# Mean-embedding projection: where block 5 is loaded, how many weight blocks load before the hold, and which engine empties the banks until tile 2 joins

## The chip, the cores and the metric

The kernel runs on one core of a Trainium2 chip. The metric is the device time of one execution in microseconds (us). It works with five engines: TensorE (PE, with PEld for its weight loads), VectorE (DVE), ScalarE (ACT), GpSimd (POOL) and SyncE (SP), which here only issues DMAs.

## The reference

```python
valid = sequence_ids < emb_table.shape[0]          # 1024 x 200 ids, 12500 items
safe_ids = jnp.where(valid, sequence_ids, 0)
seq_emb = emb_table[safe_ids] * valid[..., None]   # rows of 512 floats
denom = jnp.maximum(valid.sum(axis=1, keepdims=True), 1.0)
user_repr = seq_emb.sum(axis=1) / denom            # 1024 x 512
logits = user_repr @ proj_w + proj_b               # 512 x 12500, bias of 12500
```

The ids are drawn between 35 and 109962, so that only about 23 of a user's 200 ids are valid. The result is 1024 x 12500 floats.

## The kernel before

**Tiles and units.** The 1024 users are 8 tiles of 128. The weights are cut into 25 blocks of 500 columns (1000 KB each). The product of one block and one tile is a *unit*: 12 matmuls of 128x500 (high half of the mean by high half of the weights, high by low, low by high, four parts of 128 rows each) into one of six PSUM banks. There are 200 units, and TensorE runs them in the order of the list `units`, counted by `r`. Units are done as tiles become ready: tile 0 alone for r = 0 to 9, tile 1 *joins* at r = 10, tile 2 at 22, tile 3 at 35, tile 4 at 51 (`joined`). Blocks are counted by `q` from 0 to 46, because a tile that joins late needs the first blocks again.

**Means.** For each tile GpSimd gathers 26 *columns* (row c of each of 128 users, `gather`, L353) and one more for the rest into a ring of 12 buffers `rows`. Columns are summed by VectorE (`add_column`, L561), and for the first three tiles also by TensorE (`sum_column`, L791): all 26 of tile 0, columns 18 to 25 of tile 1 (numbers 44 to 51), 24 and 25 of tile 2 (76 and 77). TensorE's columns of tile t come at r = joined[t] - 2; then ScalarE scales the part from PSUM (`rest_share`, L449), VectorE finishes the mean (`mean_of`, L607), and TensorE turns it (`turn`, L763) at r = joined[t] - 1, between two units.

**Weights.** SyncE loads a raw block q into a slot (`load_w`, L289), ScalarE makes its high half (`w_high`, L422), VectorE the low half (`w_low`, L625, two instructions, after which the raw slot is free). Block 0 to 4 are prepared ahead; block q >= 5 at the step `split_due[q]`: blocks 5 to 10 at r = 1 to 6, 11 to 14 at r = 11 to 14, 15, 16, 17 at r = 23, 24, 25, 18 at 36. Slots: two in `w_raw` (slots 0, 1), two in the area of the means (`raw_at_hi`, `raw_at_lo`, slots 2, 3), and one in `stage`, used once (slot 4, block 4). From block 16 (`MORE_LOADS`) only slots 0 and 1 are used. A load waits (`raw_last`) for the low half of the block that had its slot before. The loads of `first_loads` (q = 0 to 8) are issued ahead of the unit loop; from q = `LATE_LOAD` = 7 on they are held until the last column of tile 0 has landed. Later loads are issued at the step where the block before in their slot is split.

**Leaving the banks.** A finished unit is copied to `stage` and stored. It leaves by ScalarE if `by_act[r]` (L413, and then TensorE adds the bias with a thirteenth matmul, L847, from `bias_parts`), else by VectorE (L640, which adds `bias_sb`, a ring of four bias blocks that SyncE loads from step `BIAS_DUE` = 3). `by_act` holds for all r below joined[ACT_TILES] = 10 and for the even r below 65. Unit r waits until unit r - 6 has left its bank.

Each engine does its instructions in the order written. In VectorE's loop at step r: `move_out(r)` if it is its unit, `fill_slots` at a join (it waits for TensorE's `list_rest`, L775 to L777, behind that unit), `w_low`, `mean_of`, and the columns due at r. In ScalarE's loop `w_high` comes ahead of `move_out(r)`. In SyncE's loop at step r: bias loads at `BIAS_DUE`, store(r), weight loads, bias loads of a slot that comes free.

Of the kernel before, what the change touches and what calls it, by code (L numbers as in the profile page):

```python
# [5 lines left out]
def mean_embedding_projection(nc, ids, table, proj, bias, out, FAST=26,  # L6
# [9 lines left out]
    K = HID // P  # L16
# [10 lines left out]
    RAW, SPLIT, BIAS, ROWS, PLACED, BANKS = 2, 5, 4, 12, 2, 6  # L27
# [1 line left out]

    ON_PE, DIAGS = ((0, FAST), (18, FAST), (24, FAST)), 4  # L30
    RAW_MORE, MORE_LOADS = 2, 16
    FURTHER_BEHIND, LIST_FIRST_AT, BIAS_DUE = 20, 21, 3
    ACT_TILES, BOTH_TILES = 1, 5
    PART_AT = (0, 32, 64)
    BIAS_ROWS = PART_AT[-1] + NB
    COLS = FAST * TILES
# [15 lines left out]
    LOADS = start[-1] + NB  # L52
# [8 lines left out]
    UNITS = len(units)  # L61
    assert UNITS == TILES * NB
    first_unit = [min(r for r, (x, _) in enumerate(units) if x == q) for q in range(LOADS)]
    last_unit = [max(r for r, (x, _) in enumerate(units) if x == q) for q in range(LOADS)]
    joined = [min(r for r, (_, x) in enumerate(units) if x == t) for t in range(TILES)]
    stores, at = [], 0
    for q, first, n in steps:
# [19 lines left out]
                      for t in range(TILES)]  # L87
    assert all(by_pe[FAST * t + j] is False and j >= FAST - ROWS for t, j in enumerate(further_behind) if t)
    GATHER_LEAD = 5
    LATE_LOAD, REST_FIRST_AT, OPENED = 7, 18, SPLIT - 1  # L90

    def column_due(c):

# [5 lines left out]


    ONCE = RAW + RAW_MORE
    raw_slot = [q if q <= ONCE else (q - 1) % ONCE if q < MORE_LOADS else q % RAW for q in range(LOADS)]
    raw_turn = [sum(raw_slot[x] == raw_slot[q] for x in range(q + 1)) for q in range(LOADS)]
    raw_last = [max((x for x in range(q) if raw_slot[x] == raw_slot[q]), default=None) for q in range(LOADS)]
    assert MORE_LOADS < JOIN[TILES // 2] and RAW_AT + BW <= (STAGE - K) * BW

    split_due = [None] * SPLIT + [min(last_unit[q - SPLIT] + 1, first_unit[q] - 1) for q in range(SPLIT, LOADS)]

    w_view = proj.rearrange("(k p) n -> p k n", p=P)
# [5 lines left out]
    with ctx:  # L115
        def sb(name, shape, dt):
            return ctx.enter_context(nc.sbuf_tensor(name, shape, dt))

        def sem(name):
            return ctx.enter_context(nc.semaphore(name))  # L120
# [63 lines left out]
        bias_sb = sb("bias_sb", [P, BIAS, BW], F32)  # L184
# [49 lines left out]
        s_fb_rows = sem("branch_rows_gathered")  # L234
        s_pool_passed = sem("pool_passed")
        s_dve_passed = sem("dve_passed")
        s_raw = [sem(f"w_loaded{i}") for i in range(RAW + RAW_MORE + 1)]
        s_bias = [sem(f"bias_loaded{i}") for i in range(BIAS)]
        s_w_hi = sem("w_hi_ready")
        s_w_lo = sem("w_lo_ready")  # L240
# [24 lines left out]
        def wait_moved(engine, r):  # L265

            engine.wait_ge(s_moved_by_act if by_act[r] else s_moved_by_dve, nth_moved[r] + 1)
# [5 lines left out]
        def raw(q):  # L273
            if raw_slot[q] == ONCE:
                return raw_once
            return w_raw[:, raw_slot[q]] if raw_slot[q] < RAW else raw_more[raw_slot[q] - RAW][:]

        def diagonal_of(c):
# [5 lines left out]
        @block.sync  # L284
        def _(sp):
            def load_w(q):
                if raw_last[q] is not None:
                    sp.wait_ge(s_w_lo, raw_last[q] + 1)
                sp.dma_start(raw(q), w_view[:, :, bass.ts(q % NB, BW)]).then_inc(s_raw[raw_slot[q]], 16)  # L289

            def load_bias(i):

                if i >= BIAS:
                    wait_moved(sp, late_last[i - BIAS])
                sp.dma_start(bias_sb[:, i % BIAS], bias_view[late[i] % NB:late[i] % NB + 1].to_broadcast([P, BW])).then_inc(
                    s_bias[i % BIAS], 16)

            def store(g):
                r, q, first, n = stores[g]
                wait_moved(sp, r + n - 1)  # L300
                sp.dma_start(out_view[:, first:first + n, bass.ts(q % NB, BW)],
                             stage[:, g % STAGE, 0:n]).then_inc(s_stored[g % STAGE], 16)

            sp.dma_start(ids_sb[:, 0], ids_view[:, 0]).then_inc(s_ids0, 16)
            sp.dma_start(ids_sb[:, 1:], ids_view[:, 1:]).then_inc(s_ids, 16)
            for q in range(RAW):
                load_w(q)
            sp.wait_ge(s_bias_zero, 1)
            for at in PART_AT:
                sp.dma_start(bias_raw[at:at + NB], bias_view).then_inc(s_bias_raw, 16)  # L310
            first_loads = [q for q in range(LOADS) if raw_last[q] is None or raw_last[q] < SPLIT]
            for q in first_loads[RAW:]:
                if q == LATE_LOAD:
                    sp.wait_ge(s_rows[(FAST - 1) % ROWS], 16 * ((FAST - 1) // ROWS + 1))
                load_w(q)
            sp.wait_ge(s_bias_parts, 3)
            for r in range(UNITS):
                if r == BIAS_DUE:
                    for i in range(BIAS):
                        load_bias(i)  # L320
                for g in range(len(stores)):
                    if stores[g][0] + stores[g][3] - 1 == r:
                        store(g)
                for q in range(len(first_loads), LOADS):
                    if split_due[raw_last[q]] == r:
                        load_w(q)
                for i in range(BIAS, len(late)):
                    if r == late_last[i - BIAS]:
                        load_bias(i)
            for i in range(STAGE):  # L330
                sp.wait_ge(s_stored[i], 16 * len(range(i, len(stores), STAGE)))
# [63 lines left out]
        def _(act):  # L395
# [20 lines left out]
            def w_high(q):  # L416
                if q >= SPLIT:
                    act.wait_ge(s_product, last_unit[q - SPLIT] + 1)
                if q == SPLIT - 1:
                    act.wait_ge(s_added, len(pe_columns[0]))  # L420
                act.wait_ge(s_raw[raw_slot[q]], 16 * raw_turn[q])
                nc.scalar.activation(w_hi[:, q % SPLIT], raw(q), ACT.Copy).then_inc(s_w_hi, 1)  # L422
# [71 lines left out]
        def _(dve):  # L494
# [120 lines left out]
            def w_low(q):  # L615
                dve.wait_ge(s_w_hi, q + 1)
                half = K // 2
                for h in range(2):
                    at = h * half
                    if q < OPENED:  # L620
                        dve.wait_ge(s_opened, 2 * q + h + 1)
                        high = acc[:, at:at + half, 0:BW]
                    else:
                        high = w_hi[:, q % SPLIT, at:at + half].bitcast(F32)
                    low = dve.tensor_tensor(w_lo[:, q % SPLIT, at:at + half], raw(q)[:, at:at + half], high, ALU.subtract)  # L625
                    if h:
                        low.then_inc(s_w_lo, 1)
                    elif q < OPENED:
                        low.then_inc(s_half_low, 1)
# [242 lines left out]
```

## Time and profile before

| what | value |
|---|---|
| median of 3 runs | 638.0 us (637.69 to 638.16) |
| the profiled execution, its own time | 639.96 us |
| its span, first to last instruction | 638.1 us |
| PE busy | 609.2 us (95%) |
| DVE busy | 407.6 us (64%) |
| ACT busy | 145.6 us (23%) |
| POOL busy | 231.1 us (36%) |
| mean granted TensorE clock | 0.997 of full speed |

The busy time of an engine is read over the span. The matmuls are pipelined and their ends are modelled, so that a busy TensorE may still have small gaps. Times within the profile count from the first instruction. The profiled execution took 1.96 us longer than the median of the runs.

### The profile page before, as it was taken

What the parts mean: (1) busy time and instruction counts of PE and PEld (TensorE: products, weight loads), DVE (VectorE), ACT (ScalarE), POOL (GpSimd) and SP (SyncE); (2) the same over time, 40 slices, a digit from 0 to 9 for tenths busy, and PEclk for the clock granted to TensorE, in tenths of its full rate; (3) what the DMA queues carried; (4) which work ended last, traced back from release to release, by engine and by line L of the source; (5) the groups of instructions that cost most, each with busy time, mean ns of one, the idle gap of its engine ahead of it and who ended that gap; (6) DMA issues with size and microseconds to landing.
All of it is one profiled execution on the core that took longest, in us unless ns stands there. A gap on an engine that the chain in (4) does not pass through costs nothing.

```text
span 638.1 us, 7597 instructions
## 1 busy us (share of the span) xinstructions
PE 609.2 (95%) x2602; PEld 477.3 (75%) x2602; DVE 407.6 (64%) x723; ACT 145.6 (23%) x161; POOL 231.1 (36%) x227
## 2 busy tenths in 40 slices
PE   1989889989999999999999999999999999999997
PEld 0337558768788787788888888888888888888886
DVE  7988949899878898697885554332333333344442
ACT  8917425132122131300200221111011111211210
POOL 5777877777763767566550000000000000000000
PEclk9998999999999999999999999999999999999999
DMA  9979999999997999798893398454555555566632
GB/s 310 387 257 342 385 394 344 358 303 324 315 302 267 311 302 315 238 325 248 253 339 114 99 293 283 123 168 163 173 167 174 177 178 177 175 191 202 218 127 103
DMA packets 77704, 158.31 MB, mean 248 GB/s; under 512 B 9288, under 2 KB 65043, under 8 KB 77659
## 3 DMA queue, kind: packets, MB, share of 16 engines
q1 hardware_dynamic: 60378, 110.30, 51.1%
q0 software_dynamic: 17280, 47.47, 22.9%
q8 instruction: 21, 0.34, 0.2%
q14 instruction: 25, 0.20, 0.1%
HBM read 115.70 MB, written 51.20 MB: 262 GB/s over the span
## 4 chain that ended last, share of the span: by engine, by line
PE 72%; DVE 19%; issue 5%; DMA 2%; DVEq 1%; ACT 0%; POOL 0%; POOLq 0%
PE acc L842 70%; DVE sums L561 7%; DVE w_lo L625 5%; DMA rows<-in_L_rec_emb_table_dram,index 2%; DVE key L518 1%; DVE top L514 1%; DVE stage L640 1%; PE acc L847 1%; DVEq L259 1%; DVE index L516 0%; PE turned L763 0%; PE turned L783 0%; DVE mean L607 0%; DMA ids_sb<-in_r_sequence_ids_dram 0%; DVE key L502 0%
## 5 line engine op out<-in xcount | busy, mean ns | idle before, releaser
L353 POOL DMA_INDIRECT rows<-in_L_rec_emb_table_dram,index x208 | 221.6, 1066 | 96.3 <-issue 55.8
L842 PE MATMUL acc<-w_hi,mean_hi 128*128 128x500 f32 x800 | 225.3, 403 | 0.8 <-ACT mean_hi L438 0.8
L640 DVE TENSOR_TENSOR stage<-acc,bias_sb 128x500 f32<-128x500 f32 x162 | 109.3, 676 | 179.2 <-PE acc L842 179.1
L842 PE MATMUL acc<-w_lo,mean_hi 128*128 128x500 f32 x800 | 214.6, 390 | 0.0
L842 PE MATMUL acc<-w_hi,mean_lo 128*128 128x500 f32 x800 | 213.7, 389 | 0.4 <-DVE mean_lo L612 0.3
L842 PEld LDWEIGHTS acc<-w_hi,mean_hi 128*128 128x128 f32 x800 | 150.7, 190 | 32.0 <-issue 4.3
L842 PEld LDWEIGHTS acc<-w_lo,mean_hi 128*128 128x128 f32 x800 | 150.8, 189 | 31.5
L842 PEld LDWEIGHTS acc<-w_hi,mean_lo 128*128 128x128 f32 x800 | 150.3, 188 | 32.1 <-DVE mean_lo L612 1.2
L561 DVE SCALAR_TENSOR_TENSOR sums<-rows,mask,sums 128x512 f32<-128x512 f32 x165 | 124.0, 752 | 16.2 <-issue 8.2
L422 ACT ACTIVATE w_hi<-w_raw 128x2000 fp32r<-128x2000 f32 x39 | 72.9, 1875 | 235.3 <-PE acc L842 215.8
L625 DVE TENSOR_TENSOR w_lo<-w_raw,w_hi 128x1000 fp32r<-128x1000 f32 x74 | 85.3, 1194 | 13.6 <-ACT w_hi L422 13.6
L413 ACT ACTIVATE stage<-acc 128x500 f32<-128x500 f32 x38 | 22.2, 587 | 79.9 <-PE acc L847 79.8
L449 ACT ACTIVATE rest_mean<-turned,inv_count 128x512 f32<-128x512 f32 x7 | 4.8, 690 | 78.3 <-PE turned L783 68.9
L791 PE MATMUL turned<-rows,diags_at_hi 128*128 128x512 f32 x30 | 15.9, 688 | 1.4 <-DMA rows<-in_L_rec_emb_table_dram,index 1.4
L514 DVE MAX8 top<-key 128x8 f32<-128x200 f32 x40 | 14.6, 366 | 0.7
L791 PE MATMUL turned<-rows,diag 128*128 128x512 f32 x20 | 10.8, 638 | 4.3 <-DMA rows<-in_L_rec_emb_table_dram,index 2.4
L847 PE MATMUL acc<-bias_parts,pick 89*128 89x500 bf16 x38 | 14.6, 385 | 0.0
L518 DVE MATCH_REPLACE8 key<-top,key 128x200 f32<-128x200 f32 x40 | 14.1, 353 | 0.0
L791 PEld LDWEIGHTS turned<-rows,diags_at_hi 128*128 128x128 f32 x30 | 6.5, 224 | 10.0 <-issue 7.3
L438 ACT ACTIVATE mean_hi<-turned 128x512 fp32r<-128x512 f32 x8 | 4.8, 598 | 32.4 <-PE turned L763 32.4
L797 PE MATMUL acc<-many,ones_b 128*128 128x16 bf16 x1 | 0.2, 194 | 12.4 <-DVE stage L659 12.4
L791 PEld LDWEIGHTS turned<-rows,diag 128*128 128x128 f32 x20 | 3.1, 188 | 11.9 <-DMA rows<-in_L_rec_emb_table_dram,index 11.8
(106 smaller groups left out, 193.1 us busy)
## 6 DMA issues: line engine op xcount, KB each, us to landing
out_dram<-stage SPq DMA_DIRECT2D x200, 250.0 KB, 3.9
w_raw<-in_L_rec_proj_w_dram SPq DMA_DIRECT2D x39, 1000.0 KB, 6.6
bias_sb<-in_L_rec_proj_b_dram SPq DMA_DIRECT2D x39, 250.0 KB, 4.9
raw_at_hi<-in_L_rec_proj_w_dram SPq DMA_DIRECT2D x4, 1000.0 KB, 11.6
rows<-in_L_rec_emb_table_dram,index POOLq DMA_INDIRECT x208, 6.0
raw_at_lo<-in_L_rec_proj_w_dram SPq DMA_DIRECT2D x3, 1000.0 KB, 15.2
stage<-in_L_rec_proj_w_dram SPq DMA_DIRECT2D x1, 1000.0 KB, 26.1
ids_sb<-in_r_sequence_ids_dram SPq DMA_DIRECT2D x1, 700.0 KB, 4.4
```

The source lines that it names most:

```text
L259: return engine.value_load(need[0:1, t + TILES:t + TILES + 1], min_val=0, max_val=MORE)
L353: return pool.indirect_dma_start(out=dst, out_offset=None, in_=table, in_offset=bass.IndirectOffsetOnAxis(ap=column, axis=0), bounds_check ...
L413: nc.scalar.activation(stage[:, g % STAGE, r - stores[g][0]], acc[:, r % BANKS, 0:BW], ACT.Copy).then_inc(s_moved_by_act, 1)
L422: nc.scalar.activation(w_hi[:, q % SPLIT], raw(q), ACT.Copy).then_inc(s_w_hi, 1)
L514: dve.max(eight, key[:]).then_inc(s_sort, 1)
L518: dve.match_replace(key[:], eight, key[:], -1.0).then_inc(s_sort, 1)
L561: dve.scalar_tensor_tensor(sums[:], rows[:, c % ROWS], mask[:, t, j:j + 1], sums[:], ALU.mult, ALU.add).then_inc(s_summed, 1)
L625: low = dve.tensor_tensor(w_lo[:, q % SPLIT, at:at + half], raw(q)[:, at:at + half], high, ALU.subtract)
L640: dve.tensor_tensor(stage[:, g % STAGE, r - stores[g][0]], acc[:, r % BANKS, 0:BW], bias_sb[:, i % BIAS], ALU.add).then_inc(s_moved_by_dve, 1)
L791: nc.tensor.matmul(turned[:], diagonal_of(c), rows[:, c % ROWS], start=j == 0, stop=j == FAST - 1).then_inc(s_added, 1)
L842: last = nc.tensor.matmul(bank, first, second, start=part + k == 0, stop=part == 2 and k == K - 1 and not by_act[r])
L847: last = nc.tensor.matmul(bank, pick[:, q % NB:q % NB + 1].to_broadcast([BIAS_ROWS, P]), bias_parts[:], start=False, stop=True)
```

## The change

The four bias buffers `bias_sb` (128 x 4 x 500 floats, as large as a raw block) become a sixth raw slot (`IN_BIAS` = 5), used once, for block 5. Blocks 6 to 15 take slots 0 to 3 in turn from slot 0 on. In the table below are the slots before and after, and which block's low half a load waits for.

| block | 5 | 6 | 7 | 8 | 9 | 10 | 11 | 12 | 13 | 14 | 15 | 16 | 17 | 18 |
|---|---|---|---|---|---|---|---|---|---|---|---|---|---|---|
| slot before | 0 | 1 | 2 | 3 | 0 | 1 | 2 | 3 | 0 | 1 | 2 | 0 | 1 | 0 |
| waits for, before | 0 | 1 | 2 | 3 | 5 | 6 | 7 | 8 | 9 | 10 | 11 | 13 | 14 | 16 |
| slot after | 5 | 0 | 1 | 2 | 3 | 0 | 1 | 2 | 3 | 0 | 1 | 0 | 1 | 0 |
| waits for, after | none | 0 | 1 | 2 | 3 | 6 | 7 | 8 | 9 | 10 | 11 | 14 | 15 | 16 |

`LATE_LOAD` goes from 7 to 8. `ACT_TILES` goes from 1 to 2, so that ScalarE empties all banks below r = 22: the six units 11, 13, 15, 17, 19 and 21 move to it, and TensorE adds their bias. The first bias loads come at r = 16 (22 - 6) in place of r = 3, after a wait for block 5's low half. 39 bias loads become 35.

```diff
-    FURTHER_BEHIND, LIST_FIRST_AT, BIAS_DUE = 20, 21, 3
-    ACT_TILES, BOTH_TILES = 1, 5
+    FURTHER_BEHIND, LIST_FIRST_AT = 20, 21
+    ACT_TILES, BOTH_TILES = 2, 5
...
-    LATE_LOAD, REST_FIRST_AT, OPENED = 7, 18, SPLIT - 1
+    LATE_LOAD, REST_FIRST_AT, OPENED = 8, 18, SPLIT - 1
...
-    raw_slot = [q if q <= ONCE else (q - 1) % ONCE if q < MORE_LOADS else q % RAW for q in range(LOADS)]
+    IN_BIAS = ONCE + 1
+    raw_slot = [q if q <= IN_BIAS else (q - 2) % ONCE if q < MORE_LOADS else q % RAW for q in range(LOADS)]
...
+    assert BIAS == K
...
-        s_raw = [sem(f"w_loaded{i}") for i in range(RAW + RAW_MORE + 1)]
+        s_raw = [sem(f"w_loaded{i}") for i in range(IN_BIAS + 1)]
...
+            if raw_slot[q] == IN_BIAS:
+                return bias_sb[:]
...
-                if r == BIAS_DUE:
+                if r == joined[ACT_TILES] - 6:
+                    sp.wait_ge(s_w_lo, IN_BIAS + 1)
                     for i in range(BIAS):
                         load_bias(i)
```

## Rows read from the trace of the kernel before

**Rows 1.** Page, part 1: busy us (share of the span) xinstructions
```profile
PE 609.2 (95%) x2602; PEld 477.3 (75%) x2602; DVE 407.6 (64%) x723; ACT 145.6 (23%) x161; POOL 231.1 (36%) x227
```
**Rows 2.** Waits of PE over the span: us in total, times, longest
```profile
PE turned L791 <- DMA rows<-in_L_rec_emb_table_dram,index: 4.3, 7, 1.4
PE turned L763 <- DVE mean L607: 2.7, 3, 1.8
...
PE acc L842 <- DVE mean_lo L612: 0.3, 1, 0.3
```
**Rows 3.** Chain that ended last: start us, us, what
```profile
80.46 5.97 DMA rows<-in_L_rec_emb_table_dram,index
86.47 1.12 PE turned L791 x2
...
354.23 280.57 PE acc L842 x1236
```
**Rows 4.** Timeline of POOL: start us, us, engine line op [idle before]
```profile
80.46 1.00 POOL L353 DMA_INDIRECT rows<-in_L_rec_emb_table_dram,index  x1 [0.30 <-issue]
```
**Rows 5.** Timeline of PE, 47 to 88 us
```profile
47.07 0.66 PE L763 MATMUL turned<-ident,mean 128*128 128x128 f32 x4 [1.49 <-DVE mean L600]
48.50 2.00 PE L842 MATMUL acc<-w_hi,mean_hi 128*128 128x500 f32 x4 [0.78 <-ACT mean_hi L438]
...
52.83 1.26 PE L842 MATMUL acc<-w_hi,mean_hi 128*128 128x500 f32 x4
...
55.78 1.25 PE L842 MATMUL acc<-w_hi,mean_hi 128*128 128x500 f32 x4
...
76.48 2.09 PE L791 MATMUL turned<-rows,diag 128*128 128x512 f32 x4 [1.83 <-ACT diag L406]
```
**Rows 6.** Windows of PE around 49 us: us, busy, clock, DMA share, GB/s
```profile
50.00:51.00 1.00, 1.00 (x4) 0.50 1.03 391
```
**Rows 7.** Timeline of DVE
```profile
46.26 0.75 DVE L600 SCALAR_TENSOR_TENSOR mean<-turned,inv_count,rest_mean 128x512 f32<-128x512 f32 x1
...
88.46 0.75 DVE L607 SCALAR_TENSOR_TENSOR mean<-sums,inv_count,rest_mean 128x512 f32<-128x512 f32 x1 [6.47 <-ACT rest_mean L449]
...
109.01 0.67 DVE L640 TENSOR_TENSOR stage<-acc,bias_sb 128x500 f32<-128x500 f32 x1
109.60 2.30 DVE L625 TENSOR_TENSOR w_lo<-w_raw,w_hi 128x1000 fp32r<-128x1000 f32 x2
```
**Rows 8.** Timeline of DVE, 137 to 170 us
```profile
137.62 0.21 DVE L576 TENSOR_SCALAR rank<-turned,own_slot 128x1 f32<-128x1 f32 x1
...
141.26 2.30 DVE L625 TENSOR_TENSOR w_lo<-raw_at_hi,w_hi 128x1000 fp32r<-128x1000 f32 x2
...
150.07 2.30 DVE L625 TENSOR_TENSOR w_lo<-w_raw,w_hi 128x1000 fp32r<-128x1000 f32 x2
...
169.40 0.75 DVE L607 SCALAR_TENSOR_TENSOR mean<-sums,inv_count,rest_mean 128x512 f32<-128x512 f32 x1
```
**Rows 9.** Timeline of PE, 130 to 171 us
```profile
130.35 0.66 PE L763 MATMUL turned<-ident,mean 128*128 128x128 f32 x4 [1.81 <-DVE mean L607]
...
136.91 0.36 PE L777 MATMUL turned<-before,select 128*128 128x1 f32 x2
...
170.20 0.66 PE L763 MATMUL turned<-ident,mean 128*128 128x128 f32 x4 [0.73 <-DVE mean L607]
```
**Rows 10.** Timeline of ACT: high half of block 17
```profile
143.79 1.87 ACT L422 ACTIVATE w_hi<-w_raw 128x2000 fp32r<-128x2000 f32 x1
```
**Rows 11.** Landing of block 15's load, issued at 103.12 us
```profile
DMA to landing us min/median/max: 7.4/7.4/7.4
```
**Rows 12.** Landing of block 7's load, issued at 43.35 us
```profile
DMA to landing us min/median/max: 6.9/6.9/6.9
```
**Rows 13.** Landing of block 17's load, issued at 115.67 us
```profile
DMA to landing us min/median/max: 10.1/10.1/10.1
```
**Rows 14.** Landing of column 25's gather, issued at 40.30 us
```profile
DMA to landing us min/median/max: 3.0/3.0/3.0
```
**Rows 15.** Landing of all 39 loads into `w_raw`, whole span
```profile
DMA to landing us min/median/max: 5.1/6.6/18.9
```

## The prediction

> **What bounds the kernel now.** I read the page's first part, then TensorE's waits, then the chain that ended last, and then the timelines of each engine around the places that these name. TensorE is busy for 95% of the span [rows 1], and from 354 us on the chain is nothing but its unit matmuls [rows 3]: every microsecond that TensorE loses before 170 us, and does not lose already, is added to the end. TensorE's own waits after the first unit are few [rows 2]: 4.3 us for gathered rows and, at the joins, 2.7 us for the mean of VectorE, 0.3 us for a low half. So a gain can come from three places only: the stretch from 73 to 87 us, where TensorE sums columns 44 to 51 of tile 1; the 1.81 us in front of tile 2's turn at 130.35; and 0.73 us in front of tile 3's at 170.20 [rows 9]. At the first place the reader is to see that column 51 is gathered at 80.46 with GpSimd never idle but for the 0.30 us of its issue [rows 4], and that its landing 5.97 us later is what TensorE waits for [rows 3]. VectorE meanwhile idles 6.47 us ahead of tile 1's mean [rows 7]: it is not the bound there. Between 137 and 169 us VectorE has no gap except one of its own registers; it is late for tile 3, and what delays it there delays TensorE.
>
> **Part 1: block 5 in the bias buffers, eight blocks ahead of the hold.** One more megabyte stands in SyncE's queue while tile 0's last columns are gathered. Column 25, issued at 40.30, landed in 3.0 us because the queue had run empty [rows 14]; with the queue busy the nearest row is column 51's, 5.97 us [rows 3]. So column 25 lands by 46.3 in place of 43.3, TensorE ends tile 0's sum 1.1 us behind it (as it does behind column 51 [rows 3]), at 47.4, and the first mean, at 46.26 now [rows 7], starts up to 1.2 us later (0 if the queue empties in time). The held loads, at 43.35 now [rows 12], go as much later, but block 7 is no longer among them. What hides the 1.2 us: TensorE reaches column 44 with 1.83 us to wait [rows 5], and the columns behind it are bound by GpSimd's steady pace, and VectorE has its 6.47 us. I cost it at 0; without that cover it is +1.2.
>
> Blocks 6 to 9 come earlier, and the four bias loads leave the stretch from 61 to 77 us. ScalarE gets blocks 9 and 10 without waiting, so that the diagonals are not late. But the last column decides: its issue is GpSimd's pace, and its landing changes only if SyncE's queue is empty at 80 to 86 us. Blocks 10 to 14 are still issued from 61 to 78 us, each released by VectorE's split of an earlier one, and five stores between them: 6.3 MB. At half of the 391 GB/s that the DMA engines move when full [rows 6] these are 32 us, until 93; even with the light gathers of columns 46 to 51 leaving SyncE's queue two thirds, 24 us, until 85 or 86. An estimate, but the queue is busy until about when the last columns land. So I take 0, with bounds -3.0 (from the latency of column 25 [rows 14]) and 0.
>
> The Trainium skill (DMA: Bandwidth & Descriptors, Queues, rings and completion order) says that each DMA engine goes round the queues that have work, packet by packet. By that rule the depth of SyncE's queue does not matter to a gather, only whether anything is in it: the gain is 0 as long as one block is left, as in my sum; if latency went by the backlog, the two megabytes less would bring part of the 3.0 us. No row here tells the two apart.
>
> **Part 2: six units by ScalarE.** Each adds one bias matmul. An all-ScalarE unit takes 55.78 - 52.83 = 2.95 us [rows 5]; a unit without it 280.57 x 12 / 1236 = 2.72 us [rows 3]. So +0.22 us each, five of them (1.1 us) ahead of tile 2's turn, the sixth behind it. From VectorE go six moves, 0.59 us each from start to start [rows 7], five ahead of tile 2's mean: 2.95 us, of which I take back 0.35 because block 11's low half then has to wait for its high half. Tile 2's mean is ready about 2.6 us earlier and TensorE comes 1.1 us later, so its 1.81 us wait vanishes: turn at 130.35 - (1.81 - 1.1) = 129.64. The sixth bias costs 0.22 and the 0.3 us wait for the low mean [rows 2] goes: at unit 23 TensorE is 0.79 us ahead. ScalarE's six moves of about 0.6 us each fall into its idle time.
>
> **Part 3: block 17 has lost its early slot.** This is nothing that the change is named for. Before, block 17 waited for block 14's low half and was issued at 115.7 [rows 13]. Now blocks 15 and 17 share slot 1, and 17 can't be issued before VectorE has split block 15 at r = 23, two steps before 17 itself is due at r = 25. On SyncE it stands behind store 23, which is no later than that. Step by step:
> - `fill_slots` at r = 22 now starts at 137.62 without a gap [rows 8]; it waits for TensorE's list, which ended at 136.91 + 0.36 = 137.27 [rows 9] and comes 0.79 earlier. VectorE can start at 136.5: 1.1 us ahead, no more, whatever it saved before.
> - Block 15's low half ends at 141.26 + 2.30 - 1.1 = 142.5. Load 17 is issued then.
> - Its landing: block 15's load went out with the queue almost empty among heavy gathers, as this one will: 7.4 us [rows 11]. Bounds 6.9 [rows 12] and 10.1 [rows 13]. At 7.4 it lands at 149.9.
> - ScalarE's high half takes 1.87 us [rows 10]: until about 151.8. `w_low(17)` starts at 151.9 in place of 150.07 [rows 8]: +1.8, where it would have been 1.1 ahead. A stall of 2.9 us.
> - Behind it on VectorE stand the rest of tile 3's columns, then moves 27, 29, 31 and the mean at 169.40 [rows 8], with no gap to take it up. The mean is 1.8 us late, and tile 3's turn goes from 170.20 to 172.0. Behind `w_high(17)` on ScalarE stands move 26, which TensorE wants only for unit 32.
> - TensorE, 0.79 ahead, waits 0.73 + 0.79 + 1.8 = 3.3 us there.
>
> By the bounds of the landing this part ends at +1.3 or +4.5 against before; I take +1.8. It already contains all that part 2 gave.
>
> **The clock.** The first unit ran at 1.2 GHz for a while: the granted clock fell to 0.50 [rows 6] after TensorE had been idle for 1.49 and 0.78 us with 0.66 us of transposes between [rows 5]. That unit took 52.83 - 48.50 = 4.33 us in place of 2.95: 1.4 us lost. The clock stayed at 2.4 GHz after the 1.81 us gap at 130. The new gap, 3.3 us, is longer than both. Bounds 0 and +1.4; nearest row: +1.4.
>
> **The sum.** 0 + 1.8 + 1.4 = +3.2 us. In the profiled execution's own time that is 639.96 + 3.2 = 643.2; against the median of the runs, which lies 1.96 us below it, 638.0 + 3.2 = 641.2 us. Behind 172 us nothing changes: the later slots are the same, and VectorE follows TensorE's lists, so that the delay is neither grown nor given back.
>
> **The rivals.**
> - *Block 17 late, but the clock holds*: 638.0 + 1.8 = 639.8. For it: three gaps of up to 1.8 us left the clock alone.
> - *SyncE's queue runs empty before column 51's landing* (not slower): TensorE starts unit 8 up to 3.0 us earlier and everything shifts with it: 641.2 - 3.0 = 638.2, and 636.8 if the clock holds. It decides where the queue drains before 80 us. For it: two megabytes less in front of it by then; against: loads 13 and 14 go out at 74 and 78 us.
> - *Block 17 is hidden* (faster): if it landed within 7.4 - 2.9 = 4.5 us of its issue VectorE would not wait; then only part 2 is left: 0.79 + 0.73 at most, some 638.0 - 1.2 = 636.8. Against: the fastest load of a block in `w_raw` in the whole trace landed in 5.1 us [rows 15].
> - *The start passes through*: if the 1.2 us of the first mean are not covered, 641.2 + 1.2 = 642.4. Against: 1.83 us of waiting and a gather pace that does not depend on it.
>
> **How the numbers follow.** Late block with clock fall 0.41; with clock kept 0.21; queue empty 0.18 (half of it at 638.2, half at 636.8); block 17 hidden 0.08; start passes through 0.12. About 0.2% (1.3 us) is what a measurement here can tell from no change. Slower: 0.41 + 0.12 and most of 0.21, allowing for small errors of the terms (0.14): 0.67. Same: the other 0.07, 0.09 at 638.2, and part of the 636.8 cases: 0.21. Faster: 0.12. The range runs from 637.4, which takes in the queue case with the fall, to 642.6, which takes in the start and a landing of block 17 of 8.8 us; what is left out is the two cases at 636.8 and a landing of 10 us, below 0.2. The likeliest case by itself, with the clock's bounds: 639.3 to 642.6.
>
> **What would show it.** In the profile after: load 17 issued at about 142.5 and ScalarE's `w_hi` near 150 waiting for that DMA; VectorE idle some 2.9 us ahead of `w_lo` of block 17; no wait at tile 2's turn, 3.3 us at tile 3's, and a clock of 0.5 behind it; 44 bias matmuls; column 51 landing near 86.4 and unit 8 starting near 87. If unit 8 starts near 84, part 1 is wrong; if VectorE does not wait near 150, part 3 is.

## The result and the profile after

| | before | after |
|---|---|---|
| median | 638.08 us (637.69 to 638.2, 4 runs) | 643.84 us (642.85 to 644.34, 4 runs) |
| profiled execution, own time | 639.96 us | 642.85 us |
| its span | 638.1 us | 641.1 us |

The change makes the kernel slower: 1.0085 times the time before, with an interval of 1.007 to 1.01. The forecast was 641.2 us, slower. The direction is right, the time lies 1.2 us above the top of the range.

The page of after, part 1 (busy us, share of the span, instructions), beside [rows 1]:

```profile
PE 610.7 (95%) x2608; PEld 477.6 (74%) x2608; DVE 404.2 (63%) x717; ACT 148.7 (23%) x167; POOL 230.5 (36%) x227
```

Six moves went from VectorE to ScalarE, and TensorE has its six more bias matmuls. TensorE's waits in after, beside [rows 2]:

```profile
PE turned L796 <- DMA rows<-in_L_rec_emb_table_dram,index: 6.6, 9, 1.2
PE turned L768 <- DVE mean L612: 4.3, 1, 4.3
...
PE turned L768 <- DVE mean L605: 0.9, 1, 0.9
...
PE acc L847 <- DVE mean_lo L617: 0.2, 1, 0.2
```

Before, the mean at L607 was waited for three times, 2.7 us in all. After, it is waited for once, for 4.3 us: one wait that takes the place of the two at tiles 2 and 3. The timeline of TensorE in after says where, beside [rows 9] (start us, us, engine line op [idle before]):

```profile
86.25 1.46 PE L847 MATMUL acc<-w_hi,mean_hi 128*128 128x500 f32 x4
...
128.64 0.60 PE L768 MATMUL turned<-ident,mean 128*128 128x128 f32 x4
...
171.86 0.66 PE L768 MATMUL turned<-ident,mean 128*128 128x128 f32 x4 [4.34 <-DVE mean L612]
172.28 1.88 PE L847 MATMUL acc<-w_hi,mean_hi 128*128 128x500 f32 x4
173.96 1.87 PE L847 MATMUL acc<-w_lo,mean_hi 128*128 128x500 f32 x4
```

The chain that ended last leads from there back to the load of block 17 (start us, us, what):

```profile
139.03 2.31 DVE w_lo L630 x2
141.36 8.51 DMA w_raw<-in_L_rec_proj_w_dram
149.95 1.89 ACT w_hi L427
151.90 1.08 issue
152.98 1.19 DVE w_lo L630
```

It is to be read as one sentence: block 15's low half ends at 141.36, in that moment load 17 is issued, it takes 8.51 us, ScalarE makes the high half, VectorE the low half. In [rows 8] VectorE began this low half at 150.07 without having waited. In after it idled 3.95 us first (timeline of VectorE):

```profile
151.86 2.31 DVE L630 TENSOR_TENSOR w_lo<-w_raw,w_hi 128x1000 fp32r<-128x1000 f32 x2 [3.95 <-ACT w_hi L427]
```

Behind the wait TensorE's clock is down for a while. Windows of TensorE in after (stretch, us, busy, granted clock, DMA share, GB/s):

```profile
165.00:170.00 5.00, 2.52 (x12) 1.00 0.91 318
170.00:175.00 5.00, 3.14 (x11) 0.74 0.96 300
175.00:180.00 5.00, 5.00 (x24) 0.92 0.76 261
```

So far the chain is as forecast, link by link; the landing took 8.5 us where 7.4 had been taken. What does not fit is the amount: 642.85 - 639.96 = 2.9 us between the two profiled executions, but 643.84 - 638.08 = 5.8 us between the medians. The experiments had to say why, and whether block 17 is really all of it.

### The profile page after: what moved, and what is told of

Same layout as the page of the kernel before. It is cut to its first block, busy times and chain, and to the rows that moved or that the text cites. A ratio compares the mean times of both kernels' runs of the same rounds, so it can differ in the third digit from the quotient of the medians.

```text
span 641.1 us, 7605 instructions
## 1 busy us (share of the span) xinstructions
PE 610.7 (95%) x2608; PEld 477.6 (74%) x2608; DVE 404.2 (63%) x717; ACT 148.7 (23%) x167; POOL 230.5 (36%) x227
## 4 chain that ended last, share of the span: by engine, by line
PE 82%; DVE 8%; DMA 5%; issue 3%; ACT 1%; POOL 0%; DVEq 0%; POOLq 0%; ACTq 0%
PE acc L847 77%; DVE sums L566 3%; PE turned L796 3%; DMA rows<-in_L_rec_emb_table_dram,index 3%; DVE w_lo L630 2%; DMA w_raw<-in_L_rec_proj_w_dram 1%; PE acc L852 1%; PE turned L788 1%; ACT w_hi L427 1%; DVE key L523 1%; PE turned L768 1%; DVE top L519 0%; DMA ids_sb<-in_r_sequence_ids_dram 0%; DVE count L657 0%; DVE stage L645 0%
## 5 line engine op out<-in xcount | busy, mean ns | idle before, releaser
L645 DVE TENSOR_TENSOR stage<-acc,bias_sb 128x500 f32<-128x500 f32 x156 | 105.1, 675 | 183.7 <-PE acc L847 183.6
L630 DVE TENSOR_TENSOR w_lo<-w_raw,w_hi 128x1000 fp32r<-128x1000 f32 x74 | 85.2, 1193 | 14.2 <-ACT w_hi L427 14.1
L418 ACT ACTIVATE stage<-acc 128x500 f32<-128x500 f32 x44 | 25.8, 587 | 79.9 <-PE acc L852 79.9
L852 PE MATMUL acc<-bias_parts,pick 89*128 89x500 bf16 x44 | 17.0, 386 | 0.0
L852 PEld LDWEIGHTS acc<-bias_parts,pick 89*128 89x128 bf16 x44 | 4.5, 101 | 11.0 <-issue 11.0
L796 PE MATMUL turned<-rows,diags_at_lo 128*128 128x512 f32 x22 | 11.7, 660 | 0.9 <-DMA rows<-in_L_rec_emb_table_dram,index 0.8
```

Source lines behind the costliest of these rows:

```text
L418: nc.scalar.activation(stage[:, g % STAGE, r - stores[g][0]], acc[:, r % BANKS, 0:BW], ACT.Copy).then_inc(s_moved_by_act, 1)
L645: dve.tensor_tensor(stage[:, g % STAGE, r - stores[g][0]], acc[:, r % BANKS, 0:BW], bias_sb[:, i % BIAS], ALU.add).then_inc(s_moved_by_dve, 1)
L796: nc.tensor.matmul(turned[:], diagonal_of(c), rows[:, c % ROWS], start=j == 0, stop=j == FAST - 1).then_inc(s_added, 1)
L852: last = nc.tensor.matmul(bank, pick[:, q % NB:q % NB + 1].to_broadcast([BIAS_ROWS, P]), bias_parts[:], start=False, stop=True)
```

## The experiments

**Theory A**: block 17's late load is the cause. Its wait and the clock fall behind it make the whole loss, and the rest of the change is a small gain. **Theory B**: the start costs too (eight loads ahead of the hold, column 25 landing later), or the moves to ScalarE do. A second question is why the profiled execution of before lay 1.96 us above its median. Each ratio is to the kernel before, timed on the same chip in the same rounds (638.94, 638.19 and 638.26 us there in the three sets).

### 1. The kernel before once more

No edit.

> The kernel of before once more, unchanged, profiled on this chip. The first profiled execution of it took 639.96 us, 1.96 us above its median. Theory A (that execution had a loss of its own, the low clock in the first unit): a profiled execution at about 638.0 to 638.3 us shows unit 0 in about 2.95 us in place of 4.33 and a mean granted clock nearer to 1. Theory B (being profiled costs about 2 us): this one shows the same 639.9 us and the same clock in unit 0.

Median 638.47 us, ratio 0.9998 (0.9987 to 1.0008). The profiled execution took 637.72 us, span 636.0, which is 2.1 us less than the span profiled first. The clock of the first units is as low as before (granted 0.89 from 45 to 60 us in both), so it is not that. The difference is there by unit 8, which starts at 85.39 in place of 87.04. GpSimd's timelines say where it arose. The execution of before that the prediction was read from:

```profile
54.63 1.99 POOL L353 DMA_INDIRECT rows<-in_L_rec_emb_table_dram,index  x1 [0.30 <-issue]
56.92 1.27 POOL L353 DMA_INDIRECT rows<-in_L_rec_emb_table_dram,index  x1 [0.30 <-issue]
```

The second execution of the same kernel:

```profile
54.58 1.04 POOL L353 DMA_INDIRECT rows<-in_L_rec_emb_table_dram,index  x1 [0.30 <-issue]
55.93 1.00 POOL L353 DMA_INDIRECT rows<-in_L_rec_emb_table_dram,index  x1 [0.31 <-issue]
```

One gather took 1.99 us instead of 1.04, the next 1.27 instead of 1.00; GpSimd is the pace of tile 1's columns, so that this arrives at unit 8 (1.65 us later in the first execution). What VectorE did meanwhile is block 4's low half, in the first execution

```profile
53.45 2.30 DVE L625 TENSOR_TENSOR w_lo<-stage,w_hi 128x1000 fp32r<-128x1000 f32 x2
```

and in the second

```profile
53.56 2.30 DVE L625 TENSOR_TENSOR w_lo<-stage,w_hi 128x1000 fp32r<-128x1000 f32 x2
```

The phase differs by 0.16 us; the last section comes back to it. So the execution that I had read the rows from had suffered a loss that the second has not, 1.2 us of it in these two gathers. The medians of before lie between the two (638.08 to 638.94 in five sets of runs), all nearer to 637.72 but the 638.94. From here on after is compared with this second trace, whose lines for the places that matter are (TensorE, then VectorE's low halves of blocks 15 and 17):

```profile
128.46 0.66 PE L763 MATMUL turned<-ident,mean 128*128 128x128 f32 x4 [1.66 <-DVE mean L607]
168.16 0.66 PE L763 MATMUL turned<-ident,mean 128*128 128x128 f32 x4 [0.59 <-DVE mean L607]
215.37 0.60 PE L763 MATMUL turned<-ident,mean 128*128 128x128 f32 x4
...
139.37 2.30 DVE L625 TENSOR_TENSOR w_lo<-raw_at_hi,w_hi 128x1000 fp32r<-128x1000 f32 x2
148.16 2.30 DVE L625 TENSOR_TENSOR w_lo<-w_raw,w_hi 128x1000 fp32r<-128x1000 f32 x2
```

### 2. The change with block 15 in slot 2

```diff
     raw_slot = [q if q <= IN_BIAS else (q - 2) % ONCE ...]
+    raw_slot[15] = 2
```

Block 17 then waits for block 11's low half (before, it waited for block 14's), and its load goes out at 102.43 us in this run's trace (141.36 in after's). Block 15 waits for block 12's low half in place of block 11's. Nothing else is touched.

> The changed kernel with block 15 in slot 2 in place of slot 1, so that block 17 waits for block 11's low half and is issued by r = 11. Theory A (the loss is block 17's late load, with the low clock behind the wait that it makes at tile 3's turn): no wait of ScalarE for a block near 142 to 150 us, the 4.34 us wait of TensorE ahead of tile 3's turn gone to under 0.5, unit 34 in about 2.95 us, and about 5.5 us less than the changed kernel, 638.3 us. Theory B (the extra block ahead of the hold or the six bias matmuls cost it): 641 to 644 us, as the changed kernel.

Median 637.26 us, ratio 0.9976 (0.9967 to 0.9985). TensorE's timeline:

```profile
168.00 0.66 PE L769 MATMUL turned<-ident,mean 128*128 128x128 f32 x4 [0.41 <-DVE mean L613]
...
215.21 0.60 PE L769 MATMUL turned<-ident,mean 128*128 128x128 f32 x4
```

Tile 3's turn is 3.9 us earlier than in after, its wait is 0.41 us and not 4.34, and there is no clock fall: from tile 3's turn to tile 4's are 47.21 us, and 48.77 in after. One number in one slot table turns 1.0085 into 0.9976: block 17's place is the whole loss of the change, and more. Theory A holds: by B a good part of the loss would have stayed, since the start and the moves are as in after.

### 3. Only the six moves

Before, with

```diff
-    ACT_TILES, BOTH_TILES = 1, 5
+    ACT_TILES, BOTH_TILES = 2, 5
```

> The kernel of before with ACT_TILES = 2 alone (six units move to ScalarE, slots and hold as before). Theory A: +1.3 us of bias matmuls against 1.8 and 0.3 us of waits that vanish, and VectorE's lead of about 1.1 us also takes the 0.73 us wait at tile 3's turn: 636.5 us, range 636 to 637.5. Theory B (VectorE has no lead to give and the bias matmuls are paid in full): 639.3 us.

Median 637.59 us, ratio 0.9984 (0.9971 to 0.9996). The wait at tile 2's turn is gone, as forecast. What the moves bring is some 1 us, less than the 636.5 us expected (range 636 to 637.5). The trace has a wait that I had not counted, 4.04 us for ScalarE's diagonals ahead of tile 1's columns (1.83 us in [rows 5]), and the granted clock is 0.76 from 75 to 80 us behind it.

### 4. Before, with block 17 late

```diff
+    raw_slot[14], raw_slot[15] = 2, 1
```

> The kernel of before with block 14 in slot 2 and block 15 in slot 1, so that block 17 waits for block 15's low half, as in the changed kernel; nothing else. Theory A (this alone makes the loss): VectorE splits block 17 about 3 us later than before, tile 3's mean comes about 3 us later, TensorE waits some 3.7 us ahead of tile 3's turn and its clock falls: 638.1 + 3 + 1.4 = 642.5 us. Theory B (it is hidden in this kernel, the loss is elsewhere): 638.1 us.

Median 644.63 us, ratio 1.0088 (1.0069 to 1.0107). The sign is as theory A has it, but the run is not as clean as meant: block 14 is in slot 2 now, where its load waits for block 11's low half in place of block 10's, and VectorE waits 1.72 us ahead of block 14's low half at 113.85. TensorE's timeline shows two losses:

```profile
130.95 1.12 PE L764 MATMUL turned<-ident,mean 128*128 128x128 f32 x4 [2.71 <-DVE mean L608]
...
173.97 0.66 PE L764 MATMUL turned<-ident,mean 128*128 128x128 f32 x4 [2.76 <-DVE mean L608]
```

Tile 2's turn is 2.5 us later than in the second trace of before, with its own fall of the clock, and carries that to 173.97. Only the second part, 2.34 us of VectorE waiting ahead of block 17's low half, is what the edit was made for. The run shows that the late block alone harms a kernel without the rest of the change; its size can't be taken from the median.

### 5. The change once more

No edit.

> The changed kernel once more, unchanged, profiled again. Theory A (the missing part of the size is the base: the profiled execution of before had lost 1.6 us up to unit 8 that its usual executions don't lose): unit 8 starts at 86.3 us or up to 1 us later, tile 3's turn at 172 to 173 behind a wait of 4 us or more, unit 34 at the low clock, own time 643.5 to 644.5. Theory B (the changed kernel loses something in its other executions that its first profile doesn't show, up to 1.5 us behind 172 us): the stretch from tile 3's turn to the end is longer than the 469.2 us of the first profile.

Median 644.36 us (643.18 to 646.06), ratio 1.0099 (1.008 to 1.0117). In the profiled execution, 644.08 us, tile 3's turn is at 171.83, as in the first (171.86). But tile 4's is at 221.80 and not 220.63. TensorE's windows in it:

```profile
170.00:175.00 5.00, 3.17 (x10) 0.61 0.93 302
175.00:180.00 5.00, 5.00 (x18) 0.71 0.67 225
```

The clock stays down longer than in the first trace: 221.80 - 171.83 = 49.97 us to tile 4's turn against 47.21 without a fall, which is 2.76 us; the first trace has 48.77 - 47.21 = 1.56. Nearly the same wait (4.34 and 4.61 us) costs 1.6 us of clock in one execution and 2.8 in another. Theory A's signs are all there. Theory B's is too: from tile 3's turn to the end are 470.5 us against 469.2, and 1.2 of the 1.3 us between are this longer fall.

### 6. and 7. Work put into the gap

After, with matmuls ahead of tile 3's turn that use a free bank which unit 34 then overwrites; 12 in the first kernel, 18 in the second.

```diff
+                if r + TURN_AHEAD == joined[3]:
+                    wait_moved(pe, r - BANKS)
+                    for m in range(12):
+                        nc.tensor.matmul(acc[:, r % BANKS, 0:BW], mean_hi[:, 0, 0:P], w_hi[:, units[r][0] % SPLIT, m % K],
+                                         start=True, stop=True)
```

> The changed kernel with 12 extra matmuls of 128x500 ahead of tile 3's turn, into the bank of unit 34, which that unit then overwrites: they stand for about 2.7 us of the 4.3 us wait and are no part of the result. Theory A (the wait costs twice, once as a wait and once by the clock): the turn comes as late as in the changed kernel, but unit 34 takes 2.95 us in place of 4.5 and the time falls by 1.5 us, to about 642.3. Theory B (the slow unit 34 has another cause, its weights or VectorE): 643.8 us with unit 34 at 4.5 us, or longer by what the extra matmuls delay.

> As the kernel with 12 extra matmuls ahead of tile 3's turn, but with 18 (4.1 us; no part of the result). With 12 the wait left behind them was 2.8 us in the profile and the clock still fell. Theory A (the idle time itself brings the clock down): with under 1.6 us left the clock holds in most executions, unit 34 takes 2.95 us, the stretch from tile 3's turn to tile 4's is 47.2 us, and the median is 641.5 to 642.5. Theory B (the clock falls whatever fills the wait, because of what stands around it): 643 to 644.4 us.

With 12 matmuls: median 642.97 us, ratio 1.0073 (1.0057 to 1.0089). Six executions took 642.26, 642.27, 642.44, 643.51, 644.21 and 644.33 us; the profiled one is the 644.21:

```profile
167.48 2.86 PE L828 MATMUL acc<-w_hi,mean_hi 128*128 128x500 f32 x12
173.16 0.66 PE L768 MATMUL turned<-ident,mean 128*128 128x128 f32 x4 [2.82 <-DVE mean L612]
```

2.82 us of idling were still left (load 17 landed in 9.6 us here, and the turn came 1.3 us later than in after), and tile 4's turn came 48.79 us later: the clock had fallen all the same. With 18 matmuls: median 642.45 us, ratio 1.0063 (1.0041 to 1.0086). Four executions lie between 642.42 and 642.73, the fifth, which is the profiled one, at 644.68:

```profile
167.31 4.25 PE L828 MATMUL acc<-w_hi,mean_hi 128*128 128x500 f32 x18
173.62 0.84 PE L768 MATMUL turned<-ident,mean 128*128 128x128 f32 x4 [2.07 <-DVE mean L612]
...
222.42 0.60 PE L768 MATMUL turned<-ident,mean 128*128 128x128 f32 x4
```

Here even 2.07 us were followed by a fall (48.80 us to tile 4's turn). The other four are 2.2 us faster than this one and 1.9 us faster than experiment 5's median. That is about what a clock fall costs. They have no trace, but the mean granted clock of each execution was measured. It is 0.992 to 0.995 in all ten executions of after. With 18 matmuls it is 1.000 in two of the four faster ones, and with 12 it is 0.999 in the three that took 642.26 to 642.44 us; a trace with a single fall has 0.997 (second trace of before). So in these five executions no such fall took place, neither at tile 3's turn nor elsewhere. In the other two fast ones with 18 (0.997 and 0.995) there was a fall, and where is not known. The wait itself is not touched by the filling, and some 642.4 us, 4.2 above before, is what is left with it alone.

### 8. The change without its moves

After, with `ACT_TILES` = 1. The first bias loads then come at r = 4.

```diff
-    ACT_TILES, BOTH_TILES = 2, 5
+    ACT_TILES, BOTH_TILES = 1, 5
```

> The changed kernel with ACT_TILES = 1: slots, hold and six raw buffers as changed, but units 11 to 21 as before; the first bias loads then come at r = 4. Theory A (moving the six units was worth about 1.0 us ahead of tile 3, and the late block costs 3 to 4 us and the clock whatever stands before it): tile 2's turn has its 1.7 us wait again, VectorE reaches block 15 about 1 to 2 us later, tile 3's turn at 173 to 174, 645 us. Theory B (the six moves cost by their bias matmuls): 642.5 us.

Median 646.56 us, ratio 1.0133 (1.0112 to 1.0155). TensorE waits at tile 2's turn again, and more at tile 3's:

```profile
129.75 0.66 PE L768 MATMUL turned<-ident,mean 128*128 128x128 f32 x4 [2.12 <-DVE mean L612]
...
175.57 1.12 PE L768 MATMUL turned<-ident,mean 128*128 128x128 f32 x4 [5.54 <-DVE mean L612]
```

The moves are worth 2.2 us here, about twice of what experiment 3 shows: VectorE's step at r = 22 and 23, which frees slot 1, comes later without them (block 15's low half at 141.54 and not 139.03), and with it load 17. A part of this is the clock: behind the 2.12 us wait at tile 2's turn it is 0.66 from 130 to 135 us, and 1.00 in after. Tile 3's turn is 1.6 us later than the 174 that I had allowed for; load 17 took 9.6 us to land.

### 9. Block 15 in slot 2, seven blocks ahead of the hold

Experiment 2 with

```diff
-    LATE_LOAD, REST_FIRST_AT, OPENED = 8, 18, SPLIT - 1
+    LATE_LOAD, REST_FIRST_AT, OPENED = 7, 18, SPLIT - 1
```

> The kernel with block 15 in slot 2 and LATE_LOAD back at 7: block 7 waits for the last column of tile 0 again. Theory A (the extra block makes column 25 land at 46.3 in place of 43.3 and the first unit start 1.35 us later, which the columns of tile 1 hide): first unit at 48.5, unit 8 still between 85.3 and 87, and 637.3 us, as with the hold at 8. Theory B (the start passes through): 636.0 us.

Median 636.74 us, ratio 0.9975 (0.9966 to 0.9984); experiment 2 had 0.9976. Unit 8 starts at 85.98 and in experiment 2 at 86.53. The eighth block ahead of the hold neither costs nor brings anything that these medians can tell.

### 10. The slots of before, with the moves and the later bias loads

Before, with

```diff
-    FURTHER_BEHIND, LIST_FIRST_AT, BIAS_DUE = 20, 21, 3
-    ACT_TILES, BOTH_TILES = 1, 5
+    FURTHER_BEHIND, LIST_FIRST_AT, BIAS_DUE = 20, 21, 16
+    ACT_TILES, BOTH_TILES = 2, 5
```

> The kernel of before with ACT_TILES = 2 and the bias loads from r = 16 on (BIAS_DUE = 16); slots as before, so no sixth raw buffer and block 17 early. Theory A (the late bias loads and the six moves are what is worth having, the block in the bias buffers is not): blocks 9 and 10 land 2 to 4 us earlier than with ACT_TILES = 2 alone, TensorE's 4.0 us wait for the diagonals is under 2, and the time is 636.7 us, as the kernel with block 15 in slot 2 and the hold at 7. Theory B (the sixth buffer is worth something): 637.6 us, as with ACT_TILES = 2 alone.

Median 636.71 us, ratio 0.9971 (0.9957 to 0.9985), as good as experiments 2 and 9. The block in the bias buffers, the part that the change is named for, is worth nothing that can be measured. TensorE's waits in this kernel:

```profile
PE turned L791 <- ACT diag L406: 2.5, 2, 2.0
```

and in experiment 3, where the bias loads stay at r = 3:

```profile
PE turned L791 <- ACT diag L406: 4.0, 1, 4.0
```

The two waits don't measure the bias loads. TensorE comes to these columns 1.5 us earlier in experiment 3's trace (72.16 against 73.66), because its clock held in the first unit there. ScalarE's first diagonals come only 0.55 us sooner with the later loads (76.14 against 76.69), and at 74.82 in the second trace of before, which has the loads at r = 3. Theory A's 2 to 4 us for blocks 9 and 10 were not seen, and the intervals of 0.9971 and 0.9984 overlap: that the later bias loads bring anything is not shown.

## Why the prediction was right in kind and too small

Each place in after, beside the second trace of before and the forecast:

| place | before, second trace | forecast | after | after, second trace |
|---|---|---|---|---|
| unit 8 starts | 85.39 | 87 | 86.25 | 86.16 |
| tile 2's turn, wait ahead | 128.46, 1.66 | 129.64, 0 | 128.64, 0 | 128.32, 0 |
| load 17 issued | early (115.67 in the first trace) | 142.5 | 141.36 | 141.06 |
| its landing takes | | 7.4 | 8.5 | 8.6 |
| low half of block 17, wait ahead | 148.16, 0 | 151.9, 2.9 | 151.86, 3.95 | 151.66, 4.05 |
| tile 3's turn, wait ahead | 168.16, 0.59 | 172.0, 3.3 | 171.86, 4.34 | 171.83, 4.61 |
| tile 3's turn to tile 4's | 47.21 | 1.4 more | 48.77 | 49.97 |

**The step that failed is "the sum".** I had +3.2 us against the profiled execution, and between the two profiled executions it was +2.9. But I carried it over to the median as a constant: "against the median of the runs, which lies 1.96 us below it, 638.0 + 3.2". The 1.96 us were not a constant. They were a loss of that one execution, 1.2 us of it in the two gathers at 54.63 and 56.92 us, and after shared only a part of it. From an execution of before without it (637.72 us) the same places of after are 171.86 - 168.16 = 3.70 us later at tile 3's turn, plus 1.56 of clock, minus 0.16 for the rest: 5.1 us, the difference of the spans (641.1 - 636.0). The forecast had hit absolute times of one trace (172.0 against 171.86) and missed the difference between kernels. The hit was luck: load 17 was issued 1.1 us earlier than forecast, in the main because after did not have the first trace's loss, and it landed 1.1 us later than forecast.

**Part 3 (block 17)** was right in every link of its chain, not in the sizes, and it is the whole loss (experiment 2). Its size against the second trace of before is +3.7 in place of +1.8. Of the 1.9 us between, 1.1 are the landing (8.5 us where I took 7.4; within my bounds of 6.9 to 10.1; 8.6, 9.6, 9.6 and 10.2 in the traces of experiments 5, 6, 8 and 7), and 0.8 are that VectorE reached block 15's low half only 0.34 us earlier than before (139.03 against 139.37) where I had 1.1.

**Part 1 (the start)** was taken at 0 with bounds of -3.0 and 0. Column 25 landed in 6.0 us, at 46.30, and the first turn came 1.4 us later (48.41 against 47.02), about as forecast. What hid it was not the 1.83 us of waiting that I had counted on, but the clock. TensorE's wait ahead of the first turn was 0.94 us in place of 1.46, the clock stayed up, and the first unit took 2.84 us in place of 4.40. TensorE's window of after:

```profile
50.00:55.00 5.00, 5.00 (x23) 1.00 1.03 382
```

So TensorE came to tile 1's columns no later than before (73.49 against 73.68), which I had not foreseen. That the part is near 0 is luck as far as this goes. The first unit kept its clock in all six traces with eight blocks ahead of the hold, and in one of six with seven; that the shorter wait is the reason is likely, not shown. Against the second trace of before unit 8 is 0.9 us later, which is about the 0.8 us just named, and it comes by a way that I had not seen: not through TensorE's columns, but through one gather of tile 1, described in the last section. In the other traces too unit 8 starts later with eight blocks ahead of the hold (86.11 to 86.53 in six) than with seven (85.39 to 85.98 in five, not counting the trace that the forecast was read from), yet experiments 2 and 9 have the same ratio. So the rival "the start passes through" is true of single traces by less than 1 us, and of the median nothing is shown.

**Part 2 (the six moves)** came as forecast: no wait at tile 2's turn. Alone it is worth 1.0 us (experiment 3); with the later bias loads the median is 1.8 us below before (experiment 10). In the change part 3 eats it.

**The clock** fell, as taken. I had sized it as +1.4 by the first unit; two traces of after show 1.56 and 2.76. The median of after lies 1.0 us above its first profiled execution, and runs from 642.85 to 646.06 in both sets; a part of that is the length of this fall.

Sizes in sum: 1.9 us by part 3's terms, 0.2 to 1.4 by the clock. The 2.6 us between the forecast's +3.2 and the measured +5.8 lie within these.

The Trainium skill (DMA: Bandwidth & Descriptors, Queues, rings and completion order) says that each DMA engine goes round the queues that have work, a packet at a time; the rival was that the depth of SyncE's queue matters. By that rule the gathers get no faster from two megabytes less in the queue, and the traces agree: column 51's gather took 5.5 us to land in after and 5.5 us in the second trace of before, neither near the 3.0 us of [rows 14], and experiment 10, without that block, is as fast.

**Open** is why load 17 takes 8.5 to 10.2 us in the five traces with the change's slots where block 15's took 7.4 [rows 11]. Right behind it stand a bias load, a store and load 18. The timeline of SyncE's queue in after:

```profile
141.36 0.39 SPq L293 DMA_DIRECT2D w_raw<-in_L_rec_proj_w_dram  x1
141.80 0.51 SPq L299 DMA_DIRECT2D bias_sb<-in_L_rec_proj_b_dram  x1
142.35 0.43 SPq L305 DMA_DIRECT2D out_dram<-stage  x1
145.10 0.38 SPq L293 DMA_DIRECT2D w_raw<-in_L_rec_proj_w_dram  x1
```

That they share the bandwidth would be a reason, but it can't be all: in experiment 4's trace a bias load, a store and load 18 stand behind load 17 at the same distances, and it landed in 6.9 us.

## What to carry to other kernels

When a ring of buffers gets a new member, write out for every later block which block's release its load now waits for, up to the place where the numbering changes: here one entry near that place cost some 7 us (ratio 1.0085 against 0.9976) in a change that was about another block. Before a sum is set against a median, find out where the profiled execution lost or won its difference to it, by a second execution of the same kernel if there is one; if that is not known, the difference belongs into the range and not into the sum. A wait of TensorE can cost its clock on top, here 1.6 to 2.8 us behind waits of 4.3 to 4.6 us.

## What the runs showed of the hardware

**A gather's issue waits for VectorE's low half.** In all twelve traces the gather at about 54.6 us starts while VectorE makes block 4's low half, two instructions of 1.19 us (page of after: 1193 ns) that both read two operands from SBUF. VectorE's timeline of after has

```profile
54.36 2.30 DVE L630 TENSOR_TENSOR w_lo<-stage,w_hi 128x1000 fp32r<-128x1000 f32 x2
```

and GpSimd's

```profile
54.65 1.78 POOL L358 DMA_INDIRECT rows<-in_L_rec_emb_table_dram,index  x1 [0.30 <-DVE rest_index L588]
56.73 1.00 POOL L358 DMA_INDIRECT rows<-in_L_rec_emb_table_dram,index  x1 [0.30 <-issue]
```

| trace | gather's start behind the low half's | gather takes | gather's end behind the low half's start |
|---|---|---|---|
| after | 0.29 | 1.78 | 2.07 |
| experiment 6 | 0.47 | 1.60 | 2.07 |
| experiment 10 | 0.82 | 1.25 | 2.07 |
| before, second trace | 1.02 | 1.04 | 2.06 |
| before, first trace | 1.18 | 1.99 | 3.17 |
| experiment 4 | 1.19 | 1.98 | 3.17 |

In the other six traces the gather starts 0.29 to 1.00 behind and ends 2.06 or 2.07 behind.

Up to a start of 1.02 the gather ends 2.06 or 2.07 us behind the start of the first instruction, as if it had waited until that one ended and then taken 0.9 us. From a start of 1.18, when the second instruction is running, it ends 1.1 us later, as if it waited for that one. So 0.16 us of phase cost 0.95 us at once, and this decided between the two traces of before; the start of the change shifted the low half from 53.56 to 54.36 and cost 0.74 us in the same way. No run changed the low half alone, so that the mechanism rests on this regularity and on one contrast within the traces: the low halves of blocks 0 to 3 are the same instruction, but read the high half from PSUM (`acc`), and they hold no gather up. In after (VectorE, then GpSimd):

```profile
33.06 2.29 DVE L630 TENSOR_TENSOR w_lo<-raw_at_hi,acc 128x1000 fp32r<-128x1000 f32 x2
...
33.80 1.00 POOL L358 DMA_INDIRECT rows<-in_L_rec_emb_table_dram,index  x1 [0.30 <-issue]
```

This gather starts 0.74 behind the low half and takes 1.00 us; behind a low half with both operands in SBUF it would take 1.33 by the table.

The Trainium skill (SBUF — State Buffer, 🔬 SBUF: two separate sides) says that VectorE and GpSimd share one pair of ports by an exclusive lock, held for a whole instruction, which a VectorE operation with two SBUF inputs takes against a GpSimd operation that reads SBUF. The traces agree in both points, the two inputs and the wait for a whole instruction. The other way round they show no wait: the low half at 53.56 in the second trace of before starts while the gather of 53.28 (1.00 us) runs, and still takes 2.30 us.

**The clock falls after shorter waits than I had rows for.** [rows 5] had a fall after 1.49 and 0.78 us with transposes between, and [rows 9] none after 1.81. The traces add falls after 2.07 (experiment 7), 2.12 (experiment 8, tile 2's turn), 2.71 (experiment 4), 2.82 (experiment 6), 4.04 (experiment 3, ahead of tile 1's columns) and 4.3 to 5.5 us, and none after 1.66 (second trace of before) and 1.99 (experiments 4 and 10, ahead of the columns). The length of one wait does not settle it. Ahead of the first unit 1.53 and 0.78 us left the clock up in experiment 3, and 1.37 to 1.49 and 0.78 us brought it down in the five other traces with seven blocks ahead of the hold. In experiment 6 the granted clock was 0.70 from 80 to 85 us, among column sums with no wait longer than 0.82 us before it. And with the waits partly filled it held in five executions of experiments 6 and 7 and fell in both that were profiled.
